# Sixteen heads' first row maxima in two sets of PSUM banks, and alternate banks for the last attention: a transformer layer on one Trainium2 core

## The reference

```python
# attention, 16 heads of 32, sequence 512
qkv = layernorm(x) @ w_attn + b_attn
q, k, v = split into heads; q, k = rotate(q), rotate(k)   # the angle depends on the head
scores = where(causal, q @ k.T, -inf)
o = (softmax(scores) * 512 ** -0.5) @ v
x = x + layernorm(o @ w_proj + b_proj)
# feed-forward, 512 -> 2048 -> 512, ternary weights: sign(round(w / (mean|w| + eps))) * mean|w|
h = gelu(bitlinear(layernorm(x), w_fc))
x = x + layernorm(bitlinear(h, w_proj))
```

## Time and profile before

| | us |
|---|---|
| median of three executions | 1322.21 (1320.95 to 1322.66) |
| the profiled execution | 1322.04 |
| its span, first to last instruction | 1320.3 |
| first stage, until the last value remainder | about 88 |
| step 0's ten maxima, until the transpose of `mx` | 88 to 114 |
| step 7's attention, until the last head's output | 1157 to 1220 |
| step 8 | 1247 to 1320 |

### The profile page before, as it was taken

The page is one execution under the profiler, slowest core; times in us unless marked ns, Lnnn a source line. Parts: engine busy times, 40 slices in busy tenths (PEclk is TensorE's granted clock), DMA queues, the critical chain, the costliest instruction groups (busy, mean ns, idle before and its releaser), DMA issues.

```text
span 1320.3 us, 24729 instructions
## 1 busy us (share of the span) xinstructions
PE 1192.8 (90%) x9300; PEld 650.0 (49%) x9300; DVE 992.8 (75%) x2884; ACT 766.9 (58%) x1410; POOL 574.8 (44%) x634
## 2 busy tenths in 40 slices
PE   6577789999999999999999999999999999988796
PEld 4123444555545554555545554555545554554352
DVE  4666976978887787968887887968887887776532
ACT  5418654666466755666466755666465755575470
POOL 1520602871159312971259313961259213961252
PEclk9786879999999999999999999999999999989799
DMA  8420221002300222012300222012300230001000
GB/s 327 126 97 2 49 69 45 1 18 68 109 1 3 57 62 76 1 24 68 104 1 2 57 80 58 1 26 66 104 1 2 57 89 16 2 9 49 9 1 32
DMA packets 47614, 65.08 MB, mean 49 GB/s; under 512 B 8549, under 2 KB 33157, under 8 KB 46087
## 3 DMA queue, kind: packets, MB, share of 16 engines
q1 hardware_dynamic: 47494, 63.51, 16.3%
HBM read 29.63 MB, written 8.39 MB: 29 GB/s over the span
## 4 chain that ended last, share of the span: by engine, by line
PE 53%; DVE 31%; ACT 9%; issue 3%; POOL 2%; DMA 1%; POOLq 0%; SPq 0%; DVEq 0%; ACTq 0%
PE gen L468 19%; PE down L511 17%; DVE score L1076 9%; PE pv L565 4%; PE score L537 4%; DVE hT L969 4%; DVE probs L969 2%; PE score L543 2%; PE gen L528 1%; DVE mx L1076 1%; POOL rstd L1402 1%; DVE qkn L1168 1%; DVE bn L1105 1%; ACT probs L817 1%; ACT qkn L761 1%
## 5 line engine op out<-in xcount | busy, mean ns | idle before, releaser
L1402 POOL TENSOR_TENSOR rstd<-veps,mhalf 128x1 f32<-128x1 f32 (+1 forms) x104 | 67.0, 645 | 503.9 <-DVE veps L1153 363.8
L817 ACT ACTIVATE probs<-score 128x512 f16<-128x512 f32 (+1 forms) x384 | 201.7, 525 | 130.5 <-PE score L537 130.4
L969 DVE TENSOR_TENSOR probs<-score,probs 128x512 f16<-128x512 f32 (+1 forms) x384 | 212.9, 595 | 64.3 <-ACT score L819 64.2
L468 PE MATMUL gen<-x2T,t1T 128*128 128x512 f16 x1024 | 242.5, 382 | 4.0 <-ACT x2T L760 2.5
L511 PE MATMUL down<-t2T,hT 128*128 128x512 f16 x1024 | 233.0, 380 | 3.5 <-DVE xn L1138 3.5
L819 ACT ACTIVATE score<-score 128x512 f32<-128x512 f32 (+1 forms) x384 | 204.5, 532 | 0.0
L468 PE MATMUL gen<-xT,wa 128*128 128x512 f16 x768 | 180.8, 387 | 4.0 <-DVE mx L1076 4.0
L1076 DVE CUSTOM_DVE_ANT_0 score<-score,mask_rows 128x512 f32<-128x512 f32 (+1 forms) x344 | 157.8, 521 | 0.0
L969 DVE TENSOR_TENSOR hT<-gen,hT 128x512 f16<-128x512 f32 x160 | 108.6, 685 | 64.0 <-ACT gen L780 25.3
L511 PEld LDWEIGHTS down<-t2T,hT 128*128 128x128 f16 x1024 | 96.5, 98 | 110.4 <-DVE xn L1138 4.7
L468 PEld LDWEIGHTS gen<-x2T,t1T 128*128 128x128 f16 x1024 | 95.4, 98 | 109.3 <-ACT x2T L760 5.2
(11 more groups left out here) (128 smaller groups left out, 1799.2 us busy)
## 6 DMA issues: line engine op xcount, KB each, us to landing
qk<-qkn SPq DMA_DIRECT2D x384, 64.0 KB, 2.0
xo<-x SPq DMA_DIRECT2D x8, 1024.0 KB, 5.6
hT<-x SPq DMA_DIRECT2D x8, 1024.0 KB, 6.5
out<-xn SPq DMA_DIRECT2D x32, 256.0 KB, 2.2
hT<-w_fc SPq DMA_DIRECT2D x4, 1024.0 KB, 13.9
hT<-w_down SPq DMA_DIRECT2D x4, 1024.0 KB, 5.4
t2T<-w_qk SPq DMA_DIRECT2D x2, 1024.0 KB, 8.5
probs<-w_v SPq DMA_DIRECT2D x1, 1024.0 KB, 18.8
```

The source lines that it names most:

```text
L468: mm = nc.tensor.matmul(bank[:, :], a, b, start=(start and n == 0), stop=(stop and n == len(pairs) - 1))
L817: nc.scalar.activation(probs[:, h % 2, HI, 512 * i:512 * i + n], score[i][:, 0:n], ACT.Exp, scale=1.0 / S_UP)
L969: return V.tensor_tensor(out, whole, hi, ALU.subtract)
```

## The change

1. All sixteen first maximum passes run in the first stage; step 0's loop over 16 blocks is gone. Heads with an even number use the score banks, heads with an odd number three general banks, named `first max` in the plan.
2. In the first stage each of the four query and key groups has a buffer of its own: two in `qkn`, one in `x2T`, one in `xn`. ScalarE no longer waits for stacks there, but in step 0 it waits for the last stack before it normalises into `xn`.
3. The value weights are loaded before w_fc and converted earlier; the value blocks are computed in two halves, with an even head's pass between. x blocks are transposed between the second and third rotation, and all rotations wait for the identity's copies.
4. The four bias products go one by one behind queries and keys, into `pv` instead of `down`. The projection's bias and low weights move on VectorE from the first stage into step 0, behind `halve_maxima` and two x blocks.
5. The statistics of batch 1 are computed in the first stage. Two of w_down's magnitudes move to the end of the first stage, the third to the head of step 0. SyncE issues all four stacks first, then the four loads of w_down.
6. In step 7 the odd heads' scores lie in the general banks. The twelve down pieces go one to a head, into heads 0, 1, 2, 4, 7 to 10 and 12 to 15; row blocks 1 and 2 are finished at heads 6 and 11.

```diff
+LAST_DOWN_AT = {h: [divmod(n + 4, 4)] for n, h in enumerate((0, 1, 2, 4, 7, 8, 9, 10, 12, 13, 14, 15))}
+LAST_FINAL_AT = {6: 1, 11: 2}
+FIRST_MAX = {h: [("first max", 3 * h + i) for i in range(3)] for h in range(1, HEADS, 2)}
+FIRST_USES = (ROT[0:2] + XT[0:2] + ROT[2:4] + XT[2:4] + ROT[4:8] + QK[0:6] + FIRST_MAX[1] + QK[6:8] + FIRST_MAX[3]
+              + [("v", 0)] + FIRST_MAX[5] + [("v", 1)] + FIRST_MAX[7] + [("v", 2)] + FIRST_MAX[9] + [("v", 3)]
+              + FIRST_MAX[11] + FIRST_MAX[13] + FIRST_MAX[15])
+def scores_in_general(h, nxt):
+    return not nxt and h % 2 == 1 and h < HEADS
...
+        first_qkn = (qkn[:, 0, :, :], qkn[:, 1, :, :], x2T[:, 0, :, :],
+                     xn[:, :, :].rearrange("p r e -> p (r e)").bitcast(f16).rearrange("p (k t) -> p k t", k=4))
...
# SyncE, first stage
                     load_x(1)
-                    stack(0)
-                    stack(1)
-                    load_down(0)
-                    stack(2)
-                    load_down(1)
-                    stack(3)
-                    load_down(2)
-                    load_down(3)
+                    for g in range(4):
+                        stack(g)
+                    for i in range(PIECES):
+                        load_down(i)
...
# TensorE, scores(h)
-                    bank = claim_score(("scores", h), 0)
+                    in_general = scores_in_general(h, nxt)
+                    full = g_full if in_general else s_full
+                    def claim_part(i):
+                        return claim("scores", 3 * h + i) if in_general else claim_score(("scores", h), i)
+                    bank = claim_part(0)
...
# TensorE, first stage
+                    pe.wait_ge(ident_copy, 2)
+                    rotate(0)
+                    rotate(1)
                     x_turn(0)
                     x_turn(1)
-                    rotate(4)
-                    rotate(5)
+                    rotate(2)
+                    rotate(3)
                     x_turn(2)
                     x_turn(3)
+                    for n in range(4, 8):
+                        rotate(n)
                     bias_columns()
                     queries_keys(0, 0)
                     queries_keys(0, 1)
                     queries_keys(1, 0)
+                    value_bias_projected(0)
                     queries_keys(1, 1)
+                    value_bias_projected(1)
                     queries_keys(2, 0)
+                    value_bias_projected(2)
+                    max_pass(0, 1)
+                    queries_keys(2, 1)
+                    value_bias_projected(3)
+                    max_pass(1, 1, in_general=True)
+                    max_pass(2, 1)
                     gamma_total(0)
                     queries_keys(3, 0)
                     queries_keys(3, 1)
+                    max_pass(3, 1, in_general=True)
+                    pe.wait_ge(wv_low, 1)
+                    for tb in range(TB):
+                        bank = claim("v", tb)
+                        value_part(bank, tb, 0, 2)
+                        max_pass(2 * tb + 4, 1)
+                        value_part(bank, tb, 2, EC).then_inc(g_full, 1)
+                        max_pass(2 * tb + 5, 1, in_general=True)
+                    for h in range(2 * TB + 4, HEADS):
+                        max_pass(h, 1, in_general=(h % 2 == 1))
                     return
-                for u in range(FC):
+                if setup:
+                    pe.wait_ge(s_drained, S_FIRST)
+                    pe.wait_ge(g_drained, N_FIRST)
+                    bank = claim("shift", 0)
+                    nc.tensor.transpose(bank[:, 0:PARTS], mx[:, :], ident32[:, :]).then_inc(g_full, 1)
+                    x_turn(0)
+                    x_turn(1)
+                for u in range(0 if setup else FC):
...
                     scores(0)
+                if setup:
+                    x_turn(2)
+                    x_turn(3)
...
# ScalarE: first stage after the rotations, then the head of step 0
+                    high(wa[:, HI, :, 2 * E:3 * E], w_v_in, scale=W_UP).then_inc(wv_hi, 1)
                     queries_keys(0, 0)
                     queries_keys(0, 1)
+                    magnitudes(0, wfc_in, 0)
+                    queries_keys(1, 0)
                     magnitudes(0, wfc_in, 1)
...
                     for tb in range(TB):
                         values(tb)
+                    magnitudes(1, wdown_in, 0)
+                    magnitudes(1, wdown_in, 1)
                     return
+                if setup:
+                    act.wait_ge(stacked[3], 192)
+                    act.wait_ge(ln_ready[LX], 2)
+                    normalise(0)
+                    normalise(1)
+                    magnitudes(1, wdown_in, 2)
+                    x_turned(0)
+                    normalise(2)
+                    x_turned(1)
+                    normalise(3)
...
# VectorE: first stage from query 2 on, then the head of step 0
+                    qk_low(2, 0)
+                    maxima(0, 1)
+                    qk_low(2, 1)
+                    maxima(1, 1, in_general=True)
                     magnitude(0)
+                    maxima(2, 1)
                     thresholds(0)
+                    qk_low(3, 0)
                     large(0, 0)
+                    qk_low(3, 1)
+                    maxima(3, 1, in_general=True)
                     large(0, 1)
+                    for tb in range(TB):
+                        maxima(2 * tb + 4, 1)
+                        if tb < 2:
+                            large(0, 2 + tb)
+                        v_low(tb)
+                        maxima(2 * tb + 5, 1, in_general=True)
+                    for h in range(2 * TB + 4, HEADS):
+                        maxima(h, 1, in_general=(h % 2 == 1))
+                    return
+                if setup:
+                    halve_maxima()
+                    x_low(0)
+                    x_low(1)
+                    projection_bias()
                     projection_weights()
...
                     probs_low(0)
+                if setup:
+                    x_low(2)
+                    x_low(3)
```

More of the change, by code:

```diff
@@ L98, in general_plan @@
         uses += [("next max", 3 * STEP_MAX[h] + i) for i in range(3)] if here and nxt and h in STEP_MAX else []
+        uses += [("scores", 3 * (h + 1) + i) for i in range(3)] if here and not nxt and scores_in_general(h + 1, nxt) else []
     if here:
@@ L521, in max_pass @@
                         if in_general:
-                            bank = claim("next max", 3 * u + i)
+                            bank = claim("next max" if here else "first max", 3 * u + i)
                         else:
@@ L574, in x_turn, with value_part, values @@
                     turn(bank, lambda c: xn[:, tb % 2, PARTS * c:PARTS * (c + 1)]).then_inc(g_full, 1)
[L576 to L580, removed]
+                def value_part(bank, tb, c0, c1):
                     rows = slice(PARTS * tb, PARTS * (tb + 1))
                     cols = slice(2 * E, 3 * E)
-                    products(bank, [(xT[:, a, c, rows], wa[:, b, c, cols]) for c in range(EC)
-                                    for a, b in ((HI, HI), (HI, LO), (LO, HI))]
-                             ).then_inc(g_full, 1)
+                    return products(bank, [(xT[:, a, c, rows], wa[:, b, c, cols]) for c in range(c0, c1)
+                                           for a, b in ((HI, HI), (HI, LO), (LO, HI))], start=(c0 == 0), stop=(c1 == EC))
+                def values(tb):
+                    bank = claim("v", tb)
+                    value_part(bank, tb, 0, EC).then_inc(g_full, 1)
                 def queries_keys(g, which):
@@ L708, in iteration @@
                         queries_keys(*QK_AT[h])
-                    pieces = DOWN_AT.get(h, ()) if prev else ()
+                    pieces = (DOWN_AT if nxt or not here else LAST_DOWN_AT).get(h, ()) if prev else ()
                     if h:
@@ L806, in queries_keys @@
                         act.wait_ge(w_ready, 1)
-                    if which == 0:
+                    if which == 0 and here:
                         need(act, stacked[(g - 2) % 4], 192 * (j + 1 + (1 if g >= 2 else 0)))
-                    high(qkn[:, g % 2, 1 + which, :], bank[:, :], bias=qk_bias[:, EC * which + g:EC * which + g + 1]
+                    high((qkn[:, g % 2] if here else first_qkn[g])[:, 1 + which, :], bank[:, :], bias=qk_bias[:, EC * which + g:EC * which + g + 1]
                          ).then_inc(qk_hi, 1)
@@ L868, in iteration @@
                 if nxt and not here:
-                    for n in range(4):
-                        rotated(n)
+                    rotated(0)
+                    rotated(1)
                     act.wait_ge(ln_ready[LX], 1)
@@ L1297, in iteration @@
                         final_terms(0)
+                final_at = FINAL_AT if nxt or not here else LAST_FINAL_AT
                 for h in range(HEADS):
```

216 lines of the change are left out of this document (102 added, 114 removed).

## The result

The changed kernel took **1305.61 us** (median of four, 1304.86 to 1307.07) against 1322.43 for the kernel before: ratio 0.9875, interval 0.9863 to 0.9887. The profiled execution took 1304.86, with a span of 1303.1; 17.2 less span than before. The forecast was 1304.5. It is right in the sum, but by luck: two of its terms are wrong by some 5 us each in opposite directions, which the sum hides.

What follows compares the result with a forecast made beforehand. The prediction took the one set of score banks to bound both ends, the first maxima and the last attention. 1322.0 - 6.5 (start) - 11.0 (last attention and after) = 1304.5 us; range 1297 to 1312.

Steps and rivals of the forecast that it cites:

- (a) to (d): Start, before the thirteen-head loop: first query 25.8, stacks 32.6 to 62.2, head 0 at 45.8, thirteen heads from 62.5.
- (e): First stage, VectorE's thirteen heads: maxima, comparison passes, value remainders, 9.4 us of waits; last maximum ends at 104.8.
- (f): Transpose, halving, shift and first score bank take 5.5 us, ScalarE's queue about as late; first exponent 110.7, 9.3 earlier.
- (g): Step 0: x blocks and projection work delay VectorE's first remainders to 114.7; second exponent 116.4, start gain 6.5 us.
- rival 1: Warm start: value halves and key at full clock, start gains 11 to 12, total 1299.5; chance 0.17.
- Last attention: Odd heads' scores in other banks, single down pieces: output 10.4 us earlier, 0.6 more behind it, gain 11.0.
- the walk through heads 1 to 7: Last attention's early heads: head 6 waits for head 5's output, done at 1179.8 instead of 1181.3, 1.5 us won.
- rival 3: Last attention: weighing waits for the previous head's output, 0.5 us longer each turn; end gives 6, total 1309.5; chance 0.10.
- One of the signs that I had named for being wrong: Half-clock pieces of 3.5 us in the last attention would make the forecast wrong.
- The cause that I gave: Last attention: with odd heads in the other set, scores of h+2 need only those of h drained.
- The rule on short idle gaps: Last attention: cycling PSUM banks with small gaps makes the clock oscillate; single pieces would be worse than pairs, 1333.5.
- rival 2: Last attention: spread pieces leave TensorE at half clock, +18 us there, total 1333.5, slower; chance 0.04.

Runs made afterwards that it cites:

- One set for all: Changed kernel with all sixteen first maximum passes in the three score banks, order and place kept: 1301.52 us, ratio 0.9841 against the kernel before.
- the late second set: Changed kernel with first maxima of heads 0 to 10 in the score banks, second set only for heads 11, 13 and 15: 1299.17 us.
- The copies: Changed kernel with extra copies of one matmul, changing no value, filling TensorE's waits in the last attention: 1304.61 us, attention 59.6.
- one set with single pieces: Changed kernel with all last-attention scores in the score banks, down pieces still one to a head: 1306.98 us, attention 62.4.
- the late second set with even pieces: Changed kernel, second maxima set only for heads 11, 13 and 15, first four last-attention down pieces behind heads 0, 2, 4 and 6: 1298.08 us.

## Why the prediction was right in the sum and wrong in its terms

- **(a) to (d)** held: first query at 26.30 (25.8 forecast), stacks issued from 33.17, 41.99, 50.80 and 63.10 (32.6 to 62.2), head 0 at 46.28 (45.8), head 1 at 51.16 (50.75), the thirteen heads from 63.0 (62.5).
- **(e)** is mis-sized: 104.8 forecast for the last maximum, 101.4 measured. Waits were 6.0 and not 9.4, since one of the three value halves that wait met a half clock and not all three (6 matmuls each: 2.74 once, 1.47 twice), and the comparison passes took 5.1 together and not 6.4 (2.11, 1.70, 1.28). I had set them by the earlier trace rows's long row, and the halves by the earlier trace rows's slow one. The mechanism, the shared general banks, was as told, but I priced it without asking what the kernel would be without it. One set for all says 4 us, the late second set 5 to 6.4.
- **(f)** Both queues came together as forecast (0.21 us between them), at 106.86 and not 110.7; ScalarE's own queue was 4 us shorter since its value blocks ended sooner.
- **(g)** is right: remainders 3.8 behind the first exponent, against 4.0 by my sum, and the projection work stood where I said.
- The start thus came out near **rival 1** (warm start, 11 to 12), to which I gave 0.17. Its condition, value halves at full clock, held for two of the three.
- **Last attention**: 11.0 forecast, 4.4 + 1.5 measured. Measured from the anchor, head 7's first exponent came no earlier than before (25.45 against 25.47), and head 6 was weighed by 29.5, where it was 27.7 before and I had 26.2. Head 15's first exponent came 4.0 earlier. TensorE waits 1.58, 2.03 and 1.00 for VectorE, and its clock halves for the piece of head 4 and then for the square sums, the weighing and the piece of head 7. The step that failed is the walk through heads 1 to 7, which had every matmul at full clock. The copies put that at 2.5 us of the 6.0 that are missing up to the last output. Heads 8 to 15 start 3.38 apart on average (1175.70 to 1199.33) and not 3.15 to 3.2: weighing waits some 0.3 for the output of the head before in every second head, which is a part of rival 3, and 1.75 once, and head 13's scores come 1.79 late. The whole end, 5.9, is what **rival 3** gave (6), though only in part by its handshake. So each end came out at the price of a rival, and the two differences, +4.8 and -5.1, nearly cancel.
- One of the signs that I had named for being wrong did appear: half-clock pieces of about 3.5 us in the last attention (2.93 and 3.55). By my own test the mechanism of that term was wrong, whatever the sum said.
- Behind the last output 0.6 was forecast and 1.5 came: the eight transposes took 1.09 where they had taken 1.97, and the first 12 projection matmuls 2.76 where they had taken 3.64, since TensorE kept its clock.
- The cause that I gave, that scores of odd heads run ahead in the other set, is not what brings the gain: one set with single pieces does as well within 0.3 us. Scores of h+1 could wait for the remainders of h all along, as long as no pair of pieces stood ahead of them.
- **The rule on short idle gaps** named ahead: behind waits of 1 to 2 us TensorE's clock does fall to half in this stretch, so the Trainium skill (TensorE: Matmul & The Clock Gate, "A second HAM failure mode: psum-queue depth-cycling") bears on it; it says that small gaps in each turn of a loop over PSUM banks make the clock swing and cost throughput. The trace agrees with the direction in two places, and the price was 2.5 us and not the 18 of rival 2: from head 8 on all pieces stay at 1.89 or 1.90. That holds even behind the wait of 1.75 there, while behind the same wait of 1.74 in the late second set with even pieces the piece took 3.31. What decides between the two is not shown.

## What to carry to other kernels

A second set of buffers pays only where nothing else covers the refill, and costs where it makes two streams share banks: ask for each stretch what stands between two uses, and take the second set just there. Here one set throughout was worth 4 us against two; what the late second set adds to it is smaller than these runs can show. A long block of work ahead of a short producer delays the producer's consumer by the block's whole length: splitting blocks did what doubling buffers was meant to do. And a forecast's terms should be checked one by one against the trace even when its sum is right; here +4.8 and -5.1 cancelled.

## What the runs showed of the hardware

- Useless matmuls in waits of 1 to 2 us made what follows faster: pieces went from 3.55 and 3.38 to 1.89 us, the attention from 62.1 to 59.6 and from 61.6 to 58.3.
- The same code in front gave starts up to 2.5 us apart (before's 1153.6 and 1151.1). With after's code in front, the second half of the first value block took 1.46 us in three traces and 2.38 to 2.58 in four. What I compared by single traces there had to be compared by medians.
- A comparison pass over 128x2048 took 1.28, 1.70 or 2.11 us on VectorE within one execution. The two passes of 1.28 (at 60.42 and 78.14) fell where GpSimd stood idle, the longer ones (at 69.12 and 65.27) ran while it multiplied, for all or part of their time; I had one price for all.
